# Folding keys and values on half and quarter tiles of TensorE's array, without a block-diagonal copy

## The reference, cut to what matters

```python
x = x + _L0_xattn_ref(_layernorm(x, axis=-1), ctx_1024, ...)
x = x + _L0_ffn_ref(_layernorm(x, axis=-1), ...)
# inside _L0_xattn_ref
lat = layernorm(latents, ln_l_w, ln_l_b)
ctx = layernorm(context, ln_c_w, ln_c_b)
q = (lat @ Wq).reshape(b, n, H, D).transpose(0, 2, 1, 3)
k, v = jnp.split(ctx @ Wkv, 2, axis=-1)      # both then (b, H, s, D)
attn = jnp.clip(jnp.einsum('bhnd,bhsd->bhns', q, k) * D ** -0.5, -11.0, 11.0)
attn = jax.nn.softmax(attn, axis=-1)
out = jnp.einsum('bhns,bhsd->bhnd', attn, v)
return out.transpose(0, 2, 1, 3).reshape(b, n, INNER) @ Wo + bo
```

## Time and profile before

| | |
|---|---|
| median of 3 runs | 1436.17 us (1435.35 to 1436.32) |
| profiled execution | 1437.27 us, its span 1435.5 us |
| PE busy | 1323.5 us, 92% of the span |
| DVE busy | 1260.8 us, 88% |
| ACT busy | 642.5 us, 45% |
| POOL busy | 466.3 us, 32% |
| mean granted TensorE clock | 0.973 of 2.4 GHz |
| a step in the steady part | 47.85 to 48.00 us |

### The profile page before, as it was taken

One profiled execution on the slowest core, in us unless ns is written; L12 is line 12 of the kernel. 1 busy time (PEld: TensorE's weight loads), 2 busy tenths in 40 slices (PEclk: granted clock), 3 DMA queues, 4 the chain that ended last, 5 costly groups with the idle time before them and its releaser, 6 DMA issues.

```text
span 1435.5 us, 18514 instructions
## 1 busy us (share of the span) xinstructions
PE 1323.5 (92%) x6732; PEld 641.1 (45%) x6732; DVE 1260.8 (88%) x2187; ACT 642.5 (45%) x923; POOL 466.3 (32%) x342
## 2 busy tenths in 40 slices
PE   4872899999999999999999999689999999889997
PEld 4432445454454454544544544244444444334433
DVE  7767899999999999999999986678999999779996
ACT  1661444344434443444354432133334433398662
POOL 3002552654446526544465242000000000035555
PEclk9995999999999999999999999989999999989999
DMA  5116342444524724545256232738666653289995
GB/s 227 59 59 209 91 147 84 136 134 125 184 59 140 198 81 132 141 124 188 55 155 204 73 99 77 174 118 226 239 240 245 243 169 88 62 326 418 423 402 207
DMA packets 178428, 242.65 MB, mean 169 GB/s; under 512 B 121369, under 2 KB 140577, under 8 KB 167329
## 3 DMA queue, kind: packets, MB, share of 16 engines
q1 hardware_dynamic: 178336, 241.47, 50.9%
HBM read 121.90 MB, written 90.57 MB: 148 GB/s over the span
## 4 chain that ended last, share of the span: by engine, by line
PE 76%; DVE 7%; DMA 4%; SPq 3%; ACT 1%; issue 1%; POOL 0%; POOLq 0%; DVEq 0%; ACTq 0%
PE pg L1350 10%; PE ring L72 10%; PE ring L74 9%; PE ring L73 9%; PE pu L1356 9%; PE po L72 7%; PE po L74 7%; PE po L73 7%; PE pu L1384 5%; DMA hb<-hidden 3%; DVE w L1322 2%; ACT hb L1242 1%; SPq L1121 1%; SPq L1159 1%; PE pd L975 1%
## 5 line engine op out<-in xcount | busy, mean ns | idle before, releaser
L1225 ACT ACTIVATE sg<-pg,gate_scale 128x512 f32<-128x512 f32 x176 | 120.9, 687 | 187.6 <-PE pg L1350 187.6
L72 PE MATMUL ring<-yT,M 128*128 128x512 f16 x512 | 194.8, 381 | 4.9 <-DVE E L801 3.3
L74 PE MATMUL ring<-yT,M 128*128 128x512 f16 x512 | 195.0, 381 | 0.0
L73 PE MATMUL ring<-yT,M 128*128 128x512 f16 x512 | 194.9, 381 | 0.0
L1350 PE MATMUL pg<-xqT,w 128*128 128x512 bf16 x704 | 181.9, 381 | 2.9 <-DMA xqT<-xq 2.0
L73 PE MATMUL po<-VW,p 128*128 128x512 f16 x480 | 182.1, 379 | 0.0
L72 PE MATMUL po<-VW,p 128*128 128x512 f16 x480 | 182.1, 379 | 0.0
L74 PE MATMUL po<-VW,p 128*128 128x512 f16 x480 | 182.1, 379 | 0.0
L1356 PE MATMUL pu<-xqT,w 128*128 128x512 bf16 x704 | 181.6, 381 | 0.0
L1384 PE MATMUL pu<-w 128*128 128x512 bf16 x704 | 158.5, 386 | 18.5 <-DVE w L1324 10.1
L667 POOL TENSOR_TENSOR esum<-esum,E 128x512 f32<-128x512 f32 x96 | 134.8, 1404 | 97.8 <-DVE E L812 97.8
(11 more groups left out here) (208 smaller groups left out, 2326.5 us busy)
## 6 DMA issues: line engine op xcount, KB each, us to landing
hidden<-hb SPq DMA_DIRECT2D x11, 2816.0 KB, 8.9
hb<-hidden SPq DMA_DIRECT2D x11, 2816.0 KB, 18.1
xa<-x_rows_d SPq DMA_DIRECT2D x28, 1024.0 KB, 6.5
x<-in_x_dram SPq DMA_DIRECT2D x16, 1024.0 KB, 5.6
value_fold<-E SPq DMA_DIRECT2D x64, 256.0 KB, 2.2
VW<-value_fold SPq DMA_DIRECT2D x16, 1024.0 KB, 6.1
x_rows_d<-x SPq DMA_DIRECT2D x16, 1024.0 KB, 5.5
out_dram<-xa SPq DMA_DIRECT2D x12, 1024.0 KB, 12.5
```

Of the source, the lines that this page charges most:

```text
L72: nc.tensor.matmul(out, a_hi, b_hi, start=first, stop=False)
L73: nc.tensor.matmul(out, a_hi, b_lo, start=False, stop=False)
L74: return nc.tensor.matmul(out, a_lo, b_hi, start=False, stop=last)
L1225: nc.scalar.activation(sg[:, n % 4], pg[n % 4][:], ACT.Silu, scale=gate_scale[:, n % FT:n % FT + 1]).then_inc(silus, 1)
```

## The change

The block diagonal goes. Each head's 64 rows are matmul operands by themselves, on a part of the array that `tile_position` names. A key fold is four calls of `fold_keys`, each making two units: per head pair and product two matmuls, one on the array's upper and one on its lower 64 rows (weights 64 x 128, 64 moving columns), into two `ring` tiles. A value fold is four calls of `fold_values`, each making two units: per product four matmuls on the four 64 x 64 quarters (512 moving columns), into two `ring` tiles. For this the heads in a `ring` tile are ordered by row half (the bias's columns and the values' token order in `weights` follow). `FOLD_AFTER` puts units 0 to 3 after output tile 0 and units 4 to 7 after output tile 2. The copies, the clearing, their semaphores and one early `load_kv` go; the later ones stand after the value fold. Of `split_products`, `fold_key` and `fold_value` on ACT and DVE nothing changes.

```diff
@@ -47,6 +47,7 @@
 RSQRT_OPS = 11
 PSLOTS = 10
 UNITS = FT + DC
+SPLITS = ((0, 0), (0, 1), (1, 0))
 
 
 def rsqrt(nc, dve, y, v, t, sem, base):
@@ -148,6 +149,10 @@
         kvT = w1[:, :, :, :].rearrange("p k c n -> p k (c n)").rearrange("p k (c n) -> p k c n", n=NCTX)
 
         kv16 = w16[:, :, :, :, :].rearrange("p k a c n -> p k (a c n)").rearrange("p k (b a c s) -> p k b a c s", b=NB, a=2, s=SEQ)
+        def taken(kind, c):
+
+            return kvT[:, kind, c, :].rearrange("p (b t s) -> p b t s" if kind == 0 else "p (b s t) -> p b t s", b=NB, s=KS)
+
         def wo32(c):
 
             return w2[:, c].rearrange("p (k n) -> p k n", k=2)
@@ -355,7 +360,7 @@
                 if c == 0:
                     act.wait_ge(lo[WK + kind], DC)
                 act.wait_ge(kv_ready, n + 1)
-                nc.scalar.activation(kvT[:, kind, c, :], ps[n % 3][:], ACT.Copy, scale=kv_back[:, kind:kind + 1]).then_inc(kv_taken, 1)
+                nc.scalar.activation(taken(kind, c), ps[n % 3][:].rearrange("p (b t s) -> p b t s", b=NB, s=KS), ACT.Copy, scale=kv_back[:, kind:kind + 1]).then_inc(kv_taken, 1)
 
             def kv_high(kind, chunks=range(IC)):
                 act.wait_ge(scale_of[K + kind], 2)
@@ -501,7 +505,7 @@
 
     x_loaded = [sem(f"x_loaded{i}") for i in range(4)]
     x1_stored = [sem(f"x1_stored{i}") for i in range(4)]
-    kv_loaded, bd_zero, bd_ready = sem("kv_loaded"), sem("bd_zero"), sem("bd_ready")
+    kv_loaded = sem("kv_loaded")
     fold_spilled, fold_loaded = [sem(f"fold_spilled{k}") for k in range(4)], sem("fold_loaded")
     ln_step, ln_y, y_hi, y_lo = sem("ln_step"), sem("ln_y"), sem("y_hi"), sem("y_lo")
     y_turned = [sem("y_turned0"), sem("y_turned1")]
@@ -518,8 +522,7 @@
-    bdv = bd[:, 1].rearrange("p a q t h s -> p a q (t h s)").rearrange("p a q (h s t) -> p a q h s t", h=2, s=KS)
-    bdf = bd[:, :, :, :, :, :, :].rearrange("p k a q t h s -> p (k a q) (t h s)")
+    fold_units = fold_d.rearrange("a q r t n -> a (q r t) n").rearrange("a (h k p) n -> a k p h n", h=2, p=P)
@@ -544,11 +547,11 @@
 
         return s // 2 if s % 2 == 0 and s < NG else None
 
-    FOLD_AFTER = ((0, 1), (2, 3, 4), (5, 6, 7), ())
+    FOLD_AFTER = ((0, 1, 2, 3), (), (4, 5, 6, 7), ())
 
     def on_sync(sp):
         def load_kv(b):
-            wait(sp, bd_ready, 8 * b)
+            wait(sp, v_psum, 8 * b)
             sp.dma_start(kvb[:, :, :, :, :].rearrange("p k a c s -> p k (a c s)"), kv_d[b]).then_inc(kv_loaded, 16)
 
         def load_x(g):
@@ -568,8 +571,7 @@
                     sp.wait_ge((v_hi, v_lo)[a], 8 * b + 2 * k + 2)
                     if k == 0 and a == 0:
                         wait(sp, fold_loaded, 32 * b)
-                    sp.dma_start(fold_d[a, 2 * k:2 * k + 2].rearrange("q r t n -> (r t) q n"),
-                                 stage[:, k, a]).then_inc(fold_spilled[k], 16)
+                    sp.dma_start(fold_units[a, k], stage[:, k, a]).then_inc(fold_spilled[k], 16)
 
         def load_fold(b, s):
             wait(sp, outs, 4 * s)
@@ -626,32 +627,20 @@
                 load_fold(bv, s)
             if s > 0:
                 store_x1(s - 1)
-            bk = keys_folded_in(s)
-            if bk is not None and bk + 1 < NB:
-                load_kv(bk + 1)
+            if bv is not None and bv + 1 < NB:
+                load_kv(bv + 1)
             if s == NG - 1:
                 keep.fetch(sp)
 
     def on_gpsimd(pool):
         nc.gpsimd.memset(magic[:, 0:1], MAGIC).then_inc(magic_set, 1)
         nc.gpsimd.memset(magic[:, 1:2], -MAGIC).then_inc(magic_set, 1)
-        nc.gpsimd.memset(bd[:, 0], 0.0).then_inc(bd_zero, 1)
 
         def round_unit(u):
             n = unit_size(u)
             pool.wait_ge(f_scaled, scaled_before(u + 1))
             wait(pool, f_spilled, 16 * u)
             nc.gpsimd.tensor_scalar(quant[:, 0:n], raw[:, 0:n], MAGIC, QMAX, ALU.subtract, ALU.min).then_inc(f_rounded, 1)
-
-        def diagonal(b, kind):
-            wait(pool, (m_psum, v_psum)[kind], 8 * b)
-            for a in range(2):
-                for h in range(2):
-                    rows = slice(64 * h, 64 * h + 64)
-                    to = bd[rows, 0, a, :, :, h, :] if kind == 0 else bdv[rows, a, :, h]
-                    order = "p c (t s) -> p c t s" if kind == 0 else "p c (t s) -> p c s t"
-                    nc.gpsimd.tensor_copy(to, kvb[rows, kind, a].rearrange(order, s=KS)).then_inc(bd_ready, 1)
-                    pool.wait_ge(bd_ready, 8 * b + 4 * kind + 2 * a + h + 1)
 
         def bias(g, t):
             pool.wait_ge(ln_y, 4 * g + t + 1)
@@ -857,16 +841,6 @@
             wait(dve, f_scaled, scaled_before(u))
             nc.vector.reciprocal(inv[:, 0:n], scale).then_inc(f_known, 1)
 
-        nc.vector.memset(bd[:, 1], 0.0).then_inc(bd_zero, 1)
-        dve.wait_ge(bd_zero, 2)
-        dve.wait_ge(kv_loaded, 16)
-        for kind in range(2):
-            for a in range(2):
-                for h in range(2):
-                    at = slice(64 * h, 64 * h + 64)
-                    to = bd[at, 0, a, :, :, h, :] if kind == 0 else bdv[at, a, :, h]
-                    order = "p c (t s) -> p c t s" if kind == 0 else "p c (t s) -> p c s t"
-                    nc.vector.tensor_copy(to, kvb[at, kind, a].rearrange(order, s=KS)).then_inc(bd_ready, 1)
         def norm(g):
             norm_stats(g)
             norm_aggregates(g)
@@ -981,38 +955,53 @@
                 ins = nc.tensor.transpose(pd[:, t * P:(t + 1) * P], rexp[:, t].rearrange("p h s -> p (h s)"), keep.ident32[:])
             ins.then_inc(rden_turned, 1)
 
-        def fold_key(b, u):
-            c, half = u // 2, u % 2
-            if u == 0:
-                pe.wait_ge(bd_ready, 8 * b + 4)
-            if u >= 4:
-                pe.wait_ge(m_lo, 8 * b + u - 3)
+        def fold_keys(b, c):
+
+            u = 2 * c
+            if c == 0:
+                pe.wait_ge(kv_loaded, 16 * b + 16)
+            if c >= 2:
+                pe.wait_ge(m_lo, 8 * b + u - 2)
             elif b > 0:
-                pe.wait_ge(exps, 8 * (2 * b - 1) + 4 + u + 1)
-            out = ring[u % 4][:].rearrange("p (t q s) -> p t q s", t=KT, q=4)
-            for q in range(4):
-                pair = 4 * half + q
-                w = slice(c * P, (c + 1) * P)
-                ins = split_products(nc, out[:, :, q, :], keep.wqT16[:, 0, pair, w], keep.wqT16[:, 1, pair, w],
-                                     bdf[:, pair, :].rearrange("p (t s) -> p t s", t=KT),
-                                     bdf[:, IC + pair, :].rearrange("p (t s) -> p t s", t=KT), True, True)
-            ins.then_inc(m_psum, 1)
-
-        def fold_value(b, q):
-            if q == 0:
-                pe.wait_ge(bd_ready, 8 * b + 8)
-            if q >= 4:
-                pe.wait_ge(v_lo, 8 * b + q - 3)
+                pe.wait_ge(exps, 8 * (2 * b - 1) + 4 + u + 2)
+            w = slice(c * P, (c + 1) * P)
+            for q in range(IC):
+                for n, (i, j) in enumerate(SPLITS):
+                    for h in range(2):
+                        at = slice(64 * h, 64 * h + 64)
+                        out = ring[(u + h) % 4][:].rearrange("p (t q s) -> p t q s", t=KT, q=IC)[:, :, q, :]
+                        ins = nc.tensor.matmul(out, keep.wqT16[at, i, q, w],
+                                               kvb[at, 0, j, q, :].rearrange("p (t s) -> p t s", t=KT),
+                                               start=(n == 0), stop=(n == 2), tile_position=(64 * h, 0))
+                        if q == IC - 1 and n == 2:
+                            ins.then_inc(m_psum, 1)
+
+        def fold_values(b, k):
+
+            u = 2 * k
+            if k == 0:
+                pe.wait_ge(kv_loaded, 16 * b + 16)
+            if k >= 2:
+                pe.wait_ge(v_lo, 8 * b + u - 2)
             else:
-                pe.wait_ge(exps, 8 * (2 * b) + 4 + q + 1)
-            split_products(nc, ring[q % 4][:], bdf[:, 2 * IC + q, :], bdf[:, 3 * IC + q, :],
-                           keep.wo16[:, 0, q], keep.wo16[:, 1, q], True, True).then_inc(v_psum, 1)
+                pe.wait_ge(exps, 8 * (2 * b) + 4 + u + 2)
+            for n, (i, j) in enumerate(SPLITS):
+                for h in range(2):
+                    at = slice(64 * h, 64 * h + 64)
+                    for half in range(2):
+                        q = u + half
+                        ins = nc.tensor.matmul(ring[(u + h) % 4][64 * half:64 * half + 64, :], kvb[at, 1, i, q, :],
+                                               keep.wo16[at, j, q], start=(n == 0), stop=(n == 2), tile_position=(64 * h, 64 * half))
+                    if n == 2:
+                        ins.then_inc(v_psum, 1)
 
         def fold(s, u):
+            if u % 2 == 1:
+                return
             if keys_folded_in(s) is not None:
-                fold_key(keys_folded_in(s), u)
+                fold_keys(keys_folded_in(s), u // 2)
             elif values_folded_in(s) is not None:
```

(17 more changed lines are left out.)

## The result

The changed kernel took 1423.66 us (median of 4 runs, 1421.90 to 1425.41), beside 1436.24 for the kernel before (4 runs): a ratio of 0.9912, 95% interval 0.9894 to 0.9930. The change is faster by 12.6 us, where 3.9 were forecast and the range began at 1425. The profiled execution took 1421.97 us, its span 1420.2, against 1437.27 and 1435.5. The four runs lie in two pairs, 1421.9 and 1425.4 us; what follows is read from a profile of the first pair.

The account below looks back on a forecast made before the run. PE was taken to bound the kernel until DVE's order binds. Gains and losses by step summed to -6.0 us, tiling +2.1, together -3.9: 1433.4 us profiled, 1432.3 as median, with a range from 1425 to 1470.

Parts of the forecast that it names:

- The value steps: Steps 2 to 12 that fold values: PE idles 1.8 us for `rexp`, so each gains 0.7 us, not 2.6.
- rival 5: The clock falls in the value steps' new 1.8 us stall, 6 x 1.7 us: 1442 us; chance 0.07.
- The key steps: Steps 3 to 13 that fold keys: a pair of matmuls takes at least one load, 53 ns; each step loses 0.45 us.
- Rival 4: Key folds: loads of 64 rows at half the price, bursts 1.3 us, key steps gain 0.9: 1422 us; chance 0.08.
- Rivals 1 to 3: Folds: key loads queue, 1469, chance 0.20; nothing overlaps, about 1515, 0.06; value row halves overlap, columns don't, 1440, 0.09.
- Tiling on and off: Changing PE's tile size around bursts: nothing to 0.165 us, twice per burst; 0.165 per step taken, +2.1 us in all.
- Steps 0 and 1: End of step 0: without POOL's copies `norm_rstd` finishes earlier and PE waits less; 2.0 us gained, step 1 nothing.
- The start: Before step 0: DVE's copies go and the first key fold runs in pairs; 0.5 us gained, between -1 and 2.
- Step 14: Norms of group s+2 are gone, so `rexp` isn't late: 2.0 us gained, before the cost of tiling.
- POOL's copies at nothing in steady steps: Removing POOL's copies (7 x 8) gains nothing there: they overlap no slow DVE work and POOL is idle beside them.

Follow-up runs that it names:

- run 3: The changed kernel with DVE's reciprocal moved ahead of the layer norm statistics of group s+2: 1413.40 us, ratio 0.9844 to the kernel before.
- run 8: The changed kernel with the first burst of a step cut in two by `FOLD_AFTER`, three bursts in all: 1411.53 us, ratio 0.9830 to the kernel before.
- run 1: The kernel before with each key-fold matmul of 128 columns cut into two of 64 on the whole array, each with its own load: 1438.36 us.
- run 2: The changed kernel with the 48 upper-half matmuls of each key burst first, then the 48 lower: 1437.17 us.
- run 10: The changed kernel with DVE's reciprocals ahead of the statistics and the first burst cut in two: 1415.85 us, ratio 0.9848 to the kernel before.
- run 7: The changed kernel with the second and third groups of x loaded only after the first has landed: 1425.32 us, ratio 0.9928 to the kernel before.
- run 6: The changed kernel with ScalarE's writes of the values in `weights` in straight order, without the stride: 1423.59 us, ratio 0.9921 to the kernel before.
- run 5: The changed kernel with GpSimd's eight copies per pair of steps put back, into scratch that nothing reads: 1426.96 us, ratio 0.9941 to the kernel before.
- run 11: The changed kernel with three bursts, reciprocals first, and unread matmuls around step 0 and behind attention: 1411.53 us, ratio 0.9817 to the kernel before.
- run 9: The changed kernel with unread matmuls where TensorE stood idle around step 0 and behind the last attention group: 1421.97 us, ratio 0.9891 to the kernel before.

## Why the prediction was wrong, step by step

- **The value steps: right.** Forecast -0.7 and 0.165 for tiling, -0.53 each; measured -0.50 (-1.04 in step 12). The stall ahead of the turning back is there, 1.40 us (forecast 1.8), at full clock throughout, so rival 5 fell. The mechanism was the one given: `rexp` ends 36.2 us into step 2, against 35.1 in step 4 of the earlier trace rows (1.1 later, forecast 1.2); PE turns back 36.28 us into the step instead of 36.42; only what lies behind that is gained. Runs 3 and 8 took the stall away in two ways and got 10 and 12 us.
- **The key steps: the step that failed.** "So a pair can't be quicker than one load, 53 ns." It rested on the earlier trace rows, the difference of two records of loads (a record is how long one load is under way, not how far apart loads can follow), and on the earlier trace rows, fp32 weights. Run 1 measured 29 ns with full loads, run 2 showed the halves overlap: a pair takes at most 31. The key steps' +0.45 and 0.165 became -0.58, so 1.2 us each and, with the shorter stalls of steps 11 and 13, 8.2 us over six steps. In the terms of the profiled execution the miss is 11.4 us (1433.4 forecast, 1421.97 measured), and this is the largest part of it; the others are below, and the ffn's 2.85 and the last wait's 1.18 are in no term of the forecast. Run 2 puts the forecast's pair back: its key steps are 0.53 us longer than before's, forecast 0.61. Its total, 1437.17, is 3.8 above the forecast: its first scores come 4.4 us later than forecast (150.32), its steps 0 and 1, where the clock came back late, take 87.58, 1.6 more than forecast, and the rest is 2.2 less.
- **How near the miss was.** Two of the four runs, 1425.41 and 1425.35, lie just inside the stated range and two outside. Where the median fell is in part luck; that the key steps went down and not up is not.
- **Rival 4** named nearly the right time for a pair (28 ns) and 1422 us, with a chance of 0.08 and 0.9 us for a key step where 0.58 came, but for a wrong reason: it is not the 64 rows that make a load quick, since loads of 128 rows keep up nearly as well in run 1 (29 ns, against 27 for those of 64 rows in run 2). The Trainium skill (TensorE: Matmul & The Clock Gate, LDWEIGHTS) gives P/1.2 ns, which would be 107 ns for 128 columns; run 1's 29 ns is far below. The same page of the Trainium skill says, in its section on Fast Weight Load, that 128 weights not in fp32 are read in four chunks of 32 columns at once. The pace of run 1 and that of the fp32 weights in the earlier trace rows fit this, though no run tests it; it would have told against the failed step.
- **Rivals 1 to 3** fell with the bursts: a pair takes 31 ns at most, and six value groups of four take 1.42 us, 0.237 each.
- **Tiling on and off: right in size.** 0.09 us ahead of a burst, and 0.1 to 0.2 in it; by runs 3 and 10 one more burst costs 0.28 us, within the estimate (0 to 0.33) and above the 0.165 that was taken.
- **Steps 0 and 1**: forecast -2.0, measured -3.71. The wait ahead of step 1's scores fell from 3.27 us to 0.42, and they run at full clock. Run 7 shows 3 us of luck of the clock in the same steps: with the clock as late as there, only 0.77 would have been gained. The forecast -2.0 is neither confirmed nor refuted.
- **The start**: forecast -0.5, measured +1.56. Taking the strided write at nothing was wrong: 1.2 us instead of 0.69 for eight writes, 1.5 of the 2.4 us by which the stage ends later (run 6); the rest is open. And of the copies removed from DVE nothing was gained, since x lands 9.3 to 10.3 us behind the stage's end and the copies had lain under that wait (read from the rows; run 7 shows only that the loads beside it are not the reason).
- **Step 14**: forecast -1.8, measured -1.04; a stall of 0.87 us is still there. With the statistics gone, what makes `rexp` late is its own copy: it takes 3.18 us, from 832.16, beside GpSimd's operation on 1408 columns that starts at 830.11 (3.42 in the kernel before, where PE had slack for it). In steps 11 to 13 the copy takes 0.55 to 0.60 and a stall of 0.8 us comes from the order, as in the others.
- **POOL's copies at nothing in steady steps**: right, 0.74 us over thirteen steps (run 5).

## What to carry to other kernels

When the leading engine gets less to do, look at once at what the next engine delivers to it and in which order: here 1.4 us of each step were lost to statistics that stood ahead of a reciprocal, and a table's line gave 1.2 of them back. Price a small matmul by the distance of its starts in a row with the same type and shape, never by the record of its load; where no such row is there, the doubt belongs in the chance of a rival, and 0.08 was too little. Cutting one long burst into two pays if the consumer's chain stands behind the first; one more burst costs 0.28 us here. A slow operation beside another engine's is not yet a cause: look whether anyone waited for it.

## What the runs showed of the hardware

- Loads of 128x128 fp16 weights kept up with one matmul of 64 columns every 29 ns (run 1), while loads of the same shape have records of 100 ns.
- Two row halves of the array, each with its own 64x128 load, ran a burst in 1.50 us instead of 2.61 (the changed kernel and run 2); four quarters of 64x64 ran 24 matmuls in 1.42 us.
- ScalarE's fp32 write of 128x512 with a stride of 8 elements took 1.2 us instead of 0.69 (run 6).
- A DVE copy of 128x512 in fp32 went from 0.43 to 3.19 us beside a GpSimd operation of 4.95 us (run 10); the copy's end follows the operation's by 0.3 us.
- A wait of 1.4 us was followed by full clock in the changed kernel (steps 2 and 3, granted clock 1.00), and by matmuls at half clock for 4 us in step 13 of run 10, and of run 11 too (one every 0.43 us). The length of the wait alone doesn't tell which comes.
- After 4.66 us without work, behind 12 us of matmuls (at full clock from 130 us on), PE ran its next burst at a granted clock of 0.51 (run 9: 2.74 us for what takes 1.57 at full clock), and was at full clock again for the scores.
```profile
142.87 2.74 PE L973 MATMUL ring<-kvb,w 64*128 64x64 f16 x96 [4.66 <-DVE M L780]
```
```profile
142.80:145.60 2.80, 2.73 (x97) 2.65 (x98) 1.81 (x4) 1.12 (x3) 0.00 (x0) 0.51 0.76 150
```
